# Private banks for the maxima around a filler, tasks in parts, and an early first convolution: a four-layer sequence kernel

## What is computed

```python
x = x + attention_8_heads(x, mask=cond, Wq, Wo)        # keys = queries = values; the head's width is 32
x = x + causal_conv_over_rows(x, w=cond)               # 16 taps, w[tap, t] for column t
x = x + gru_scan(h0=cond, inputs=x, W_ih, W_hh, b)     # 256 steps over the rows, a state of 16 x 512
x = x + attention_16_heads(x, mask=cond, Wq, Wk, Wv)   # the head's width is 16
# softmax inside: att = q k / 4 + b, masked; att = exp(att - max) / sum
```

## Time and profile before

| | us |
|---|---|
| median of 3 runs | 3259.2 (3253.0 to 3263.5) |
| the profiled execution | 3255.7 |
| its span, first to last instruction | 3253.6 |

### The profile page before, as it was taken

How to read it: one execution, slowest core, us unless ns; L and a number is a source line. 1 busy time by engine, 2 the same in 40 slices (tenths; PEclk the granted TensorE clock), 3 DMA queues, 4 the chain that set the end, 5 groups by cost and what they waited for, 6 DMA issues and landing times. The chain is left out here.

```text
span 3253.6 us, 118593 instructions
## 1 busy us (share of the span) xinstructions
PE 2852.3 (88%) x48924; PEld 1557.7 (48%) x48924; DVE 1962.8 (60%) x4201; ACT 1261.7 (39%) x1987; POOL 583.4 (18%) x687
## 2 busy tenths in 40 slices
PE   6999999998399999999999999759888888888882
PEld 2333333333388888888888888612222222222210
DVE  4555555551777767676767764547666666766650
ACT  1545444543011111111111111116666767766763
POOL 0000000000011212121212211321333223333322
PEclk8999999999699999999999999968989998999986
DMA  1211101111000000000000000032344333333411
GB/s 55 84 48 46 37 33 46 46 34 31 12 1 0 0 1 0 1 0 0 0 0 0 1 0 0 1 85 66 89 120 109 99 107 109 100 96 116 113 48 64
DMA packets 129545, 146.41 MB, mean 45 GB/s; under 512 B 23574, under 2 KB 89062, under 8 KB 129426
## 3 DMA queue, kind: packets, MB, share of 16 engines
q1 hardware_dynamic: 116754, 138.77, 15.3%
q10 hardware_dynamic: 12672, 6.29, 0.7%
HBM read 100.60 MB, written 44.40 MB: 45 GB/s over the span
## 5 line engine op out<-in xcount | busy, mean ns | idle before, releaser
L1309 DVE TENSOR_REDUCE x<-bank 128x1 f32<-128x512 f32 x1024 | 639.2, 683 | 294.9 <-PE bank L1423 294.6
L1240 ACT ACTIVATE region<-exp_ps,x 128x1024 f32<-128x1024 f32 x512 | 544.6, 1111 | 133.0 <-PE exp_ps L1397 132.7
L799 PE MATMUL exp_ps<-region,gru_hT 128*16 128x128 f32 x16384 | 495.6, 273 | 0.5 <-DVE gru_hT L896 0.4
L799 PEld LDWEIGHTS exp_ps<-region,gru_hT 128*16 128x16 f32 x16384 | 431.4, 103 | 19.7 <-DVE gru_hT L896 0.9
L1423 PE MATMUL bank<-region 52*128 52x512 f16 x1024 | 304.6, 418 | 80.1 <-DVE x L1309 63.0
L834 ACT ACTIVATE gru_r<-exp_ps 128x128 f32<-128x128 f32 x256 | 71.0, 277 | 750.2 <-PE exp_ps L799 750.2
L861 DVE SCALAR_TENSOR_TENSOR xT<-x,condT,xT (+1 forms) x480 | 358.4, 795 | 1.1 <-issue 1.1
L506 DVE TENSOR_REDUCE l_maxes<-exp_ps 128x2 f32<-128x1024 f32 x176 | 215.2, 1224 | 223.4 <-PE exp_ps L567 221.0
L1410 PE MATMUL bank<-region,x 128*17 128x512 f32 x2048 | 295.1, 650 | 49.1 <-ACT x L1224 48.5
L731 POOL TENSOR_TENSOR xT<-xT,gru_hT 128x64 f32 (+1 forms) x256 | 135.6, 530 | 990.0 <-DVE gru_hT L896 645.1
L785 PE MATMUL exp_ps<-region,gru_x_st 128*32 128x128 f32 x8192 | 294.2, 274 | 0.0
(11 more groups left out here) (156 smaller groups left out, 3711.4 us busy)
## 6 DMA issues: line engine op xcount, KB each, us to landing
key_query_scratch<-x SPq DMA_DIRECT2D x96, 256.0 KB, 3.3
region<-key_query_scratch SPq DMA_DIRECT2D x128, 192.0 KB
l_rden<-rden_scratch SPq DMA_DIRECT2D x64, 256.0 KB
l_out<-x_scratch SPq DMA_DIRECT2D x64, 192.0 KB
l_xin<-in_x SPq DMA_DIRECT2D x16, 512.0 KB, 4.3
l_rden<-rden_scratch SPq DMA_DIRECT2D x128, 64.0 KB, 2.1
l_xres<-in_x SPq DMA_DIRECT2D x16, 512.0 KB, 3.7
x_scratch<-x SPq DMA_DIRECT2D x16, 512.0 KB, 10.1
```

The lines of the kernel that those rows point to most:

```text
L799: last = pe.matmul(out[QW * j:QW * j + rows, cols], hT[:, p, k, 0:rows], wh[:, k, j, gate, :], start=False, stop=True, skip_group_check=True)
L1240: act.activation(probs[:, 2 * (seg % 2) + hp, :, :], exp_ps[slot % 2][:, :, :], ACT.Exp, scale=factors[:, 2:3])\
L1309: dve.tensor_reduce(maxes[:, half, qt, head % HH:head % HH + 1], tasks.bank(n)[:, :], AX_X, ALU.max)\
```

## The change

1. **First columns' convolution.** The 64 taps of the first 32 columns are made in the first attention layer, into a free part of `region` (`first_chunk`): for batches 0 to 13 three taps behind each slot of VectorE's steps 15 and 16, for the last two batches after the last output. In `gru_part` one copy brings the result to `xT`, GpSimd's staging waits for the copy, and the four maxima of those columns are taken in the first two steps of the recurrence. GpSimd waits for maxima ahead of its additions and no longer ahead of its staging.
2. **Banks.** The maxima have two banks of their own (4 and 5), the tasks one (7). In a slot TensorE now does: scores, first maximum, the filler (a part of a task in an even slot, the weighted sums in an odd one), second maximum. Tasks `q`, `k` and `v` come in two parts, two slots apart.
3. **Slots.** `AT` gives every even slot from 2 to 30 one filler; `mta` goes from slot 16 to 22, `part1` of the query from 4 to 13, of the key from 13 to 21. The reciprocal comes ahead of slot 6's maxima, where it came behind slot 5's. ScalarE does a slot's exp first and empties the sums behind it, one slot earlier.
4. **`o_sb`** is double, by the parity of the step.
5. **Order on the queues.** SyncE stores the query's parts behind the loads of group 3 and `store_den` 0, then `store_out` 2 and 3, `store_den` 1, the key's parts. GpSimd splits the query behind `finish` 1 and the key behind `finish` 3.

```diff
 class Ring: ...
-    def __init__(self, tasks, taken, banks):
+    def __init__(self, tasks, taken, banks, place=None):
...
+def first_chunk(g):
+    return Arena(g.region[:, 4 * TC * TC * GATES * P + 2 * 3 * CC * C:]).take([P, TC, B, CW], F32)
...
 l0_part, VectorE
+            def conv_tap(bs, m, before):
+                k, tt = m // TC, m % TC
+                tap = (k - 1) % TAPS
+                acc = first[:, tt, bs, :]
+                more = acc
+                if k == 0:
+                    more = g.x1[:, tt, bs, PAD:PAD + CW]
+                else:
+                    wait(dve, conv_done, before + m - TC + 1)
+                dve.scalar_tensor_tensor(out=acc, in0=g.x1[:, tt, bs, tap:tap + CW], scalar=g.condT[:, tt, tap:tap + 1], in1=more,
+                                         op0=ALU.mult, op1=ALU.add).then_inc(conv_done, 1)
+            def conv_early(slot):
+                if slot == 0:
+                    dve.wait_ge(taken["out"], B - 2)
+                for m in range(min(3 * slot, CONV), min(3 * slot + 3, CONV)):
+                    conv_tap(slice(0, B - 2), m, 0)
...
+                    if isinstance(s, int) and s >= LAST:
+                        conv_early(SLOTS * (s - LAST) + slot)
             pipeline(dve, step, LAST + 1)
+            dve.wait_ge(taken["out"], B)
+            for m in range(CONV):
+                conv_tap(slice(B - 2, B), m, CONV)
...
 gru_part, GpSimd and VectorE
                 if more:
                     stage(pair + 1, 1 - par)
+                wait(pool, max_done, greatest)
...
-            pool.wait_ge(conv_done, CONV)
+            pool.wait_ge(copied, 1)
...
-            for m in range(CONV):
-                conv_tap(0, m)
-            for tt in range(TC):
-                greatest(0, tt)
-            chunk(0)
+            dve.tensor_copy(g.xT[:, :, :, 0:CW], first_chunk(g)).then_inc(copied, 1)
+            dve.wait_ge(copied, 1)
+            chunk(0, first=True)
...
 l3_part
-    AT = {"xn": 1, "mtb": 1, "q": 3, "q part1": 4, "k": 9, "k part1": 13, "mta": 16, "v": 18,
-          "reciprocal": 5}
+    AT = {("mtb", 0): 1, ("xn", 0): 2, ("xn", 1): 4, ("q", 0): 6, ("q", 1): 10, ("k", 0): 14, ("k", 1): 18, ("mta", 0): 22,
+          ("v", 0): 24, ("v", 1): 28}
+    PARTS = {"q": 2, "k": 2, "v": 2}
+    Q_PART1, K_PART1, RECIPROCAL = 13, 21, 6
...
-        o_sb = arena.take([P, GROUPS, T], F32)
+        o_sb = arena.take([P, 2, GROUPS, T], F32)
...
-        exp_ps, ring, o_ps = g.exp_ps, [g.bank[4], g.bank[5], g.bank[7]], g.bank[6]
+        exp_ps, max_ps, task_ps, o_ps = g.exp_ps, g.bank45, g.bank[7], g.bank[6]
...
 SyncE, step
                 if active(s, 2):
-                    wait(sp, stack_loaded[0], n(L, 2 * L))
-                    wait(sp, stack_loaded[1], n(L, 2 * L))
-                    store_parts(1, q_stored, n(2, 5))
...
                 if active(s, 0):
-                    store_den(0, n(4, 1))
+                    store_den(par, 0, n(4, 1))
+                if active(s, 2):
+                    wait(sp, stack_loaded[0], n(L, 2 * L))
+                    wait(sp, stack_loaded[1], n(L, 2 * L))
+                    store_parts(1, q_stored, n(2, 5))
+                if active(s, -1):
+                    store_out(s - 1, 2, n(4, -1))
+                    store_out(s - 1, 3, n(4, 0))
+                if active(s, 0):
+                    store_den(par, 1, n(4, 2))
                 if active(s, 2):
                     store_parts(0, k_stored, n(2, 6))
                     wait(sp, q_stored, n(16 * STORES, 48 * STORES))
...
 GpSimd, step
+                if active(s, -1):
+                    finish(s - 1, 1 - par, 0)
+                    finish(s - 1, 1 - par, 1)
                 if active(s, 2):
                     split(2 * (s + 2))
                 if active(s, -1):
-                    finish(s - 1, 0)
-                    finish(s - 1, 1)
+                    finish(s - 1, 1 - par, 2)
+                    finish(s - 1, 1 - par, 3)
                 if active(s, 2):
                     split(2 * (s + 2) + 1)
-                if active(s, -1):
-                    finish(s - 1, 2)
                 if active(s, 1):
                     split_max(2 * (s + 1), "mta", s + 2)
-                if active(s, -1):
-                    finish(s - 1, 3)
...
 ScalarE, evac_sums
-                wait(act, scaled, 4 * (s - 1) + grp + 1)
-                act.activation(o_sb[:, grp, :], o_ps[:, :], ACT.Copy).then_inc(o_taken, 1)
+                wait(act, scaled, 4 * (s - 2) + grp + 1)
+                act.activation(o_sb[:, par, grp, :], o_ps[:, :], ACT.Copy).then_inc(o_taken, 1)
...
 TensorE
+            def maxima(s, par, slot, hf):
+                h, qt = slot // TC, slot % TC
+                if slot % 16 == 0 and hf == 0:
+                    wait(pe, stack_loaded[2 * h // HH], 16 * LOADS * (s + 2))
+                wait(pe, taken["max"], 2 * (SLOTS * (s + 1) + slot) + hf - 1)
+                rows = slice(HALF * hf, HALF * hf + KMAX)
+                pe.matmul(max_ps[:, hf, :], stack[rows, 1 - par, 1, h, qt * P:qt * P + P],
+                          stack[rows, 1 - par, 0, h, :], start=True, stop=True).then_inc(ready["max"], 1)
...
                     if active(s, 0):
                         scores(s, par, slot)
-                    for n, (_, kind, idx, off, per) in tasks.at(slot):
-                        if active(s, off):
-                            tasks.free(pe, s, n)
-                            task(s, par, n, kind, idx)
+                    if active(s, 1):
+                        maxima(s, par, slot, 0)
+                    for kind, idx in AT:
+                        for part in range(PARTS.get(kind, 1)):
+                            if AT[kind, idx] + 2 * part == slot and active(s, OFF[kind]):
+                                task(s, par, kind, idx, part)
                     if slot % 2: ...
+                    if active(s, 1):
+                        maxima(s, par, slot, 1)
```

More of the change, by code:

```diff
@@ L81 @@
 class Ring:
-    def __init__(self, tasks, taken, banks):
+    def __init__(self, tasks, taken, banks, place=None):
         self.tasks, self.taken, self.banks = tasks, taken, banks
+        self.place = place or [n % len(banks) for n in range(len(tasks))]
     def bank(self, n):
-        return self.banks[n % len(self.banks)]
+        return self.banks[self.place[n]]
     def bank_of(self, kind, idx=0):
@@ L1000, in l3_part @@
         xs_in = sem("xs_in")
[L1002 to L1009 removed]
+        OFF = {"xn": 2, "q": 2, "k": 2, "v": 1, "mta": 1, "mtb": 0}
+        PER = {"xn": 2, "q": 2, "k": 2, "v": 2, "mta": 1, "mtb": 1}
+        one = Ring([(AT[k], k[0], k[1], OFF[k[0]], PER[k[0]]) for k in sorted(AT, key=AT.get)], taken, [task_ps])
         block = ctx.enter_context(nc.Block())
@@ L1241, in step @@
                            .then_inc(exp_done, 1)
+                    if slot == 1 and active(s, -1):
+                        evac_sums(s - 1, 1 - par, 3)
+                    if slot in (9, 17, 25) and active(s, 0):
+                        evac_sums(s, par, (slot - 9) // 8)
                     if slot == 0 and active(s, 2):
@@ L1266, in step @@
                         part1(2 * (s + 2))
-                    if slot == AT["k part1"] and active(s, 2):
+                    if slot == K_PART1 and active(s, 2):
                         wait(act, taken["k"], 2 * (s + 3))
@@ L1298, in step @@
                 for slot in range(SLOTS):
[L1299 to L1311 removed]
+                    for idx in range(CC):
+                        if AT["k", idx] + 2 == slot and active(s, 2):
                             wait(dve, ready["k"], 2 * (s + 2) + idx + 1)
@@ L1412, in weighted_sums, with task @@
                 last.then_inc(pv_done, 1)
-            def task(s, par, n, kind, idx):
-                out = tasks.bank(n)
-                if kind == "max":
-                    h, qt, hf = idx // 2 // TC, idx // 2 % TC, idx % 2
-                    if idx % 32 == 0:
-                        wait(pe, stack_loaded[2 * h // HH], 16 * LOADS * (s + 2))
-                    rows = slice(HALF * hf, HALF * hf + KMAX)
-                    last = pe.matmul(out, stack[rows, 1 - par, 1, h, qt * P:qt * P + P],
-                                     stack[rows, 1 - par, 0, h, :], start=True, stop=True)
+            def maxima(s, par, slot, hf):
[6 more added lines that the diff above has]
+                          stack[rows, 1 - par, 0, h, :], start=True, stop=True).then_inc(ready["max"], 1)
+            def task(s, par, kind, idx, part):
+                n = next(n for n, t in enumerate(one.tasks) if t[1:3] == (kind, idx))
+                out, parts = task_ps, PARTS.get(kind, 1)
+                if part == 0:
+                    one.free(pe, s, n)
                 if kind == "xn":
```

155 lines of the change are left out of this document (68 added, 87 removed).

## The result

The change makes the kernel slower: 3267.1 us in the median of 13 runs against 3255.9 of the kernel before, a ratio of 1.0040 (95% interval 1.0027 to 1.0054). One run of each, at 5399.7 and 4837.7, was disturbed and is left out of the ratio. The profiled execution of after is a long one: 3280.95 us, span 3278.6.

What follows compares the result with a forecast made beforehand. No engine was full: a TensorE-VectorE loop, stalled by the wait for `o_sb`, beside a loop through DMAs. Second layer +3.8 and part one -25.7 gave -21.9 against the 3259.2 median: 3237 us, range 3192 to 3283.

Steps and rivals of the forecast that it cites:

- (a): First-columns convolution moved into first attention layer: moved taps cost nothing, recurrence staging at 834.4 instead of 861.8, 27.4 us less.
- (b): Four maxima moved into the first two recurrence steps: 1.7 us late together, leaving part one 25.7 us less.
- (c): Second layer, doubled `o_sb`: ScalarE's 7.6 us wait per step and much of the slow clock go.
- (d): Second layer, two maxima banks with filler: TensorE's 32 slots take 49.0 us; steps -2 and -1 cost +3.
- (e): Second layer's next late waits: `mtb` rows 2 us, reciprocal's denominators 4.7, key's evacuation 3.5, key's `part1` for query's stores 3.9.
- (f): Query's stores moved later on SyncE: a serial chain of transfers gives the second layer's step, taken as 64.8 us.
- the chain's 64.2: Second-layer step from query's stores landing at 47.4 through `part1`, split, key's stores, stack and maxima's rows: 64.2 us.
- the forecast's own 48: Step 15 and end: SyncE can't pass on the last denominators before batch 14's third and fourth outputs, at 48 us.
- C: Rival: TensorE's waits for reciprocal and `part1` bring half clock, making it the bound at 68 to 70 us; 3279; chance 0.24.
- B: Rival: query's stores are there when `part1` comes; step 62.3 us, kernel 32 us faster, 3205; chance 0.20.
- D: Rival: new order works as plain filler, neither (e) nor (f) bites; step 57 us, kernel 3135; chance 0.06.
- E: Rival: moved taps aren't hidden or small ones cost 0.4; part one gives 13 us less, kernel 3250; chance 0.04.

Runs made afterwards that it cites:

- e1: After, with 126 already-met waits (63 instructions) ahead of VectorE's second-layer loop, putting it at place 22 as in before: 3252.4 us, 0.9992 to before.
- e2: Before, with 130 such waits (65 instructions), putting VectorE's loop at place 87 as in after: 3275.9 us, 1.0066 to before.
- e12: Before, with 64 such waits (32 instructions), putting VectorE's loop at place 54: 3256.9 us, 0.9989 to before.
- e15: After, with 256 such waits (128 instructions, a whole block), leaving VectorE's loop at place 87: 3274.3 us, 1.0053 to before.
- e9: Before with the first-columns convolution part alone, plus 126 waits putting VectorE's loop at place 22: 3226.8 us, 0.9902 to before.
- e10: e9 with the buffer of sums (`o_sb`) doubled in the old second layer: 3200.4 us, 0.9827 to before.
- e3: Before with the second attention layer's part of the change alone, VectorE's loop at place 22: 3276.9 us, 1.0071 to before.
- e6: e1 with SyncE's query stores ahead of the second pair of residual loads and first store of sums: 3279.7 us, 1.0084 to before.
- e13: e1 with the parts of query and key in buffers of their own: 3237.0 us, 0.9938 to before.
- e5: e1 with VectorE's reciprocal in slot 8 instead of 6: 3249.7 us, 0.9990 to before.
- e4: Before with the first-columns convolution part alone, VectorE's loop at place 87: 3251.7 us, 0.9984 to before.
- e7: e1 with SyncE's store and loads of the lower maxima rows ahead of the stack loads: 3258.7 us, 1.0018 to before.

## Why the prediction was wrong

Forecast were 3237 us and a faster kernel. The measured difference is +11.2 instead of -21.9, a miss of 33 us. About half of it, 16, is for instruction loads that no step of the forecast had (after less e1; up to 27 between other pairs). The other half is in e1, which has no such loads and whose stretches can be set against the forecast's: 8 too much for steps -2 and -1, 7 for steps 1 to 13, 3 for step 0, 1 for step 14 and the end, less 3 because its second layer starts 28.3 us earlier and not 25.7; 16 in all. So even without the loads the kernel would not have been faster: e1's ratio is 0.9992 (0.9981 to 1.0003). Point by point:

**(a) "They cost nothing" is the step that failed.** The work was priced rightly. The moved taps are hidden; the small ones took 12.6 us (12.8 forecast) and the copy of 2048 columns 1.23 (2.3). That staging starts at 834.6 (834.4) is in part luck: the last output came 1.3 us later than the 813.9 of before, which hid the 1.1 that the copy was shorter. VectorE's timeline at the first layer's end:

```profile
816.06 11.83 DVE L518 SCALAR_TENSOR_TENSOR region<-x,condT,region 128x64 f32<-128x64 f32 x60
...
833.30 1.23 DVE L949 COPY xT<-region 128x2048 f32<-128x2048 f32 x1 [4.96 <-DMA gru_h_swap<-in_cond]
```

Here the Trainium skill's page "VectorE: DVE Perf Modes" had the better number: its rule for copies from SBUF gave 1.1 us less than mine, and the trace agrees with it (1.23 against 2.3 - 1.1 = 1.2). What I priced at nothing was that 64 instructions became 128 in another place of the same engine's program, ahead of a loop that does not change. That cost 16 to 27 us, from some 1600 us later in the run on; e1, e2, e12 and e15 show it. The trace of before had the sign: its instruction queue is silent in the loop from 2460 to 3070 and has its 73 packets elsewhere, so the loop was held, and an edit ahead of it could change that. The Trainium skill's page "Runtime: NRT & Kernel Launch" (section "Instruction fetch mechanics") says that a jump to code that is no longer held makes the sequencer fetch it first, and e2 agrees with 2.4 to 4.1 us at each of its five jumps. The page gives blocks of 16 KB; on this queue the trace of e1 has 0.61 MB / 74 = 8.2 KB a packet, and the measurement decides. By the page's 256 instructions for 16 KB I estimate 128 instructions a packet, the block that the places above are counted in.

Small and also missed: TensorE could not start at 834.6, but waited until 838.1 for the biases, whose six loads SyncE issues last. PE's timeline:

```profile
838.09 0.30 PE L816 MATMUL exp_ps<-gru_bias,gru_ones 128*32 128x128 bf16 x4 [23.91 <-DMA gru_bias<-bias_parts]
```

**(b) Right** in size: the second layer starts 24.3 us earlier in the profiled execution (25.7 forecast) and 28.3 in that of e1, and e9 is 30.6 below the runs of before beside it.

**(c) Right** as far as it went: the wait is gone. In the old order two buffers of sums are worth 26 us (e10); in the new one no run tries them alone.

**(d) Mis-sized for steps -2 and -1**, where it is the term "+3 (0 to +6)": from the layer's start to `mtb` of step 0 after takes 134.5 us instead of 123.2, +11.3; e3 has 134.4. It lies between the first maximum of step -1 and that `mtb`: 72.4 us instead of 60.1. VectorE's and TensorE's timelines there, after:

```profile
2156.14 2.68 DVE L1353 TENSOR_REDUCE x<-bank 128x1 f32<-128x512 f32 x4 [1.84 <-PE bank L1455]
...
2158.02 2.07 PE L1471 MATMUL bank<-x 128*128 128x512 f32 x2
```

against VectorE's of before:

```profile
2202.02 14.44 DVE L1309 TENSOR_REDUCE x<-bank 128x1 f32<-128x512 f32 x24 [1.28 <-PE bank L1423]
```

Four maxima (two slots) take 2.68 + 1.84 = 4.52 us after. Between the two maxima of an even slot TensorE now does a part of a task, 2.07 us at a mean granted clock of 0.56, and VectorE runs out of filled banks meanwhile. Before had its tasks in clumps, and between them stretches such as this one with four maxima in 14.44 / 6 = 2.41. I had worked the loop out only for slots with scores and at full clock. How much of it the two banks cost and how much the even slots, no run separates.

**(e), (f) Right in mechanism, a little short.** In the reference step VectorE waits 4.1 us for the denominators (4.7 forecast) and ScalarE 3.5 for the query's stores (3.9); over the 13 steps the means are 45.4 / 13 = 3.5 and 35.8 / 13 = 2.8. The key's evacuation waits 18.6 / 13 = 1.4 instead of 3.5. The chain of the reference step keeps within 1.1 us of the forecast. Without the loads steps 1 to 13 take 65.1 (e3) and 65.3 (e1), 64.8 forecast. That 0.5 a step is the 7 us too much. The 0.6 that the forecast put on the chain's 64.2 has no row, and without it the miss would be larger. What (f) did not say is that the key's split hangs on a second branch too, only 1.8 us shorter (e6, e13). Step 0 took 55.6 to 55.8 (54.0), step 14 57.2 to 58.4 (57.7). For step 15 and the end the forecast's own 48 gives 48 - 54.1 = -6.1 where its sum has -6.4; e1 has 83.1 - 88.9 = -5.8.

**The rivals.** The sign is C's, the mechanism is not. C wanted half clock behind the reciprocal's and `part1`'s waits to make TensorE the bound. In the reference step of after the clock does fall behind the reciprocal's wait, for 6 us, but not behind `part1`'s (stretches with the granted clock, third from the right):

```profile
2684.00:2690.00 6.00, 5.79 (x19) 1.02 (x19) 2.73 (x5) 1.45 (x2) 0.00 (x0) 0.50 0.24 62
2712.00:2718.00 6.00, 4.90 (x32) 1.04 (x32) 3.91 (x7) 2.69 (x4) 2.81 (x3) 1.00 0.28 74
```

C's 68 to 70 us a step did not come (65.3 in e1, whose steps mostly end in a wait for the rows), and e1 mends 16 us without touching these waits. What the waits themselves cost is not shown, as e5 only moved them. The 0.91 of after was a consequence of the stalls at the jumps: e1 has 0.93, and e2 0.91 where before has 0.93. B's condition was made in e6 and e13. As an edit of SyncE's order (e6) it makes the kernel slower, as a second buffer (e13) it gives half of what B said (15 us of 32). D and E did not happen. The range, 3192 to 3283, held the time, because C's price reached that far and not because a case had the cause.

**Open.** By my count 277 instructions from place 87 lie in three blocks of 128, as from 22 or 54. What stands ahead of the program, and so where a block really begins, was not measured; the limit lies between 54 and 87. With 21 to 53 unseen instructions in front, the loop would reach into a fourth block from 87 and not from 54, an estimate from the places alone. Why the stall is 2.2 to 5.5 us long (after, e2, e4, e15), and why one jump of after and two of e15 show none, is open; the stack's loads (192 KB each), which SyncE issues at the same time, may lengthen it, which was not tried. The second layer's part alone (e3) costs 20.5 us, of which the terms above name the places; which of its edits causes how much was not taken apart, but for the doubled sums.

## What to carry to other kernels

Count the instructions that an edit adds to an engine's program ahead of a hardware loop, and compare the packets of the instruction queue in the loop before and after; where a loop lost its place, a few cheap instructions in idle time ahead of it can put it back (here 63). When a chain of transfers bounds a step, look for the branch next to it in length before moving anything in a queue: here a second buffer shortened one branch alone (e13), and a new order lengthened another (e6, e7). When a wait goes, look where it comes back (e5). Try the parts of a change apart: here the doubled sums alone were worth 26 us, and the banks, slots and queue orders around them, together, more than took it back (e3: 20.5 us slower).

## What the runs showed of the hardware

A loop of 277 VectorE instructions runs without instruction loads from places 22 and 54 and with five a round from place 87, where VectorE stands 2.2 to 5.5 us at most jumps back (17 of the 20 in after, e2, e4 and e15; the other three show none); the whole kernel gets 0.5 to 0.8% slower. A copy of 128 x 2048 fp32 from SBUF to SBUF took 1.23 us on VectorE, 0.60 ns a column, where 512 columns from PSUM took 0.69 us, 1.35 ns a column. Independent taps of 64 columns followed each other at 11.83 / 60 = 0.197 us.
